# A graph network layer on one core: TensorE's instructions written as loops, and a ring of 48 gathered tiles instead of 50

## The reference, cut to what matters

```python
def mish(x): return x * jnp.tanh(jax.nn.softplus(x))
sent = nodes[senders]                                # one row of 128 for each of 50000 edges
e = mish(sent + edges @ W_e_k + W_e_b)
agg = jax.ops.segment_sum(e, receivers, num_segments=n)
h = (1.0 + eps) * nodes + agg
...
# layers 1 and 2 sum neighbours again over the same src, dst:
agg = jax.ops.segment_sum(h[src], dst, num_segments=n_nodes)
```

## Time and profile before

| | us |
|---|---|
| median of 3 runs | 2208.66 |
| lowest, highest | 2203.86, 2209.03 |
| the profiled execution, its own time | 2216.36 |
| its span, first to last instruction | 2214.6 |
| build, first to last product of line 685 (about) | 75 to 485 |
| edges, first word of line 699 to last (about) | 494 to 938 |

### The profile page before, as it was taken

One profiled execution on the slowest core, in us unless ns is written; L12 is line 12 of the kernel. 1 busy time (PEld: TensorE's weight loads), 2 busy tenths in 40 slices (PEclk: granted clock), 3 DMA queues, 4 the chain that ended last, 5 costly groups with the idle time before them and its releaser, 6 DMA issues. The chain is left out here.

```text
span 2214.6 us, 31367 instructions
## 1 busy us (share of the span) xinstructions
PE 1322.1 (60%) x7890; PEld 1079.8 (49%) x7890; DVE 1066.3 (48%) x2950; ACT 944.2 (43%) x2004; POOL 1037.5 (47%) x1171
## 2 busy tenths in 40 slices
PE   3222146666676689799989997314444454434666
PEld 2100013444554578688989895214433453424555
DVE  4411149873443467554964315314444454433666
ACT  0100137774454468275536645413333343333424
POOL 5677710005566640024458441665565666556234
PEclk9555569988888789999989998657676777667787
DMA  5221212224565563074545451546667666666521
GB/s 147 70 66 53 68 55 104 90 99 152 166 197 162 169 211 101 11 252 164 194 136 208 147 209 49 162 135 172 172 184 197 199 187 197 177 169 176 157 67 43
DMA packets 214072, 314.19 MB, mean 142 GB/s; under 512 B 31232, under 2 KB 159743, under 8 KB 213818
## 3 DMA queue, kind: packets, MB, share of 16 engines
q1 hardware_dynamic: 110724, 153.96, 21.9%
q0 software_dynamic: 33488, 81.02, 13.0%
q10 hardware_dynamic: 69734, 77.65, 10.9%
HBM read 223.87 MB, written 88.67 MB: 141 GB/s over the span
## 5 line engine op out<-in xcount | busy, mean ns | idle before, releaser
L374 POOL DMA_INDIRECT fr_ring<-table,src_i x392 | 376.2, 960 | 405.5 <-SPq L655 277.7
L1765 POOL DMA_INDIRECT e_kv<-kv_table,e_idx x392 | 387.1, 987 | 269.0 <-DVE e_msg L1848 153.7
L685 PE MATMUL fe_ps<-fe_space 128*128 128x400 bf16 x591 | 176.0, 422 | 244.5 <-issue 151.9
L685 PEld LDWEIGHTS fe_ps<-fe_space 128*128 128x128 bf16 x591 | 86.0, 145 | 334.3 <-issue 309.2
L776 DVE TENSOR_SCALAR fe_space<-fe_space,fr_key 128x400 bf16<-128x400 f16 x591 | 157.5, 323 | 176.1 <-remote 77.7
L1004 POOL CAST ly_af<-ly_au 128x640 fp32r<-128x640 uint16 x240 | 163.4, 729 | 126.4 <-DVE ly_part L1409 61.0
L1779 PE MATMUL e_q<-e_qs,e_mask 128*128 128x136 f32 x784 | 148.1, 360 | 80.9 <-issue 48.2
L1831 ACT ACTIVATE e_row<-e_p 128x864 f32<-128x864 f32 x56 | 49.6, 885 | 336.4 <-remote 292.5
L731 ACT ACTIVATE fe_space<-fe_ps 128x800 uint16<-128x800 f32 x100 | 83.6, 836 | 255.8 <-PE fe_ps L685 140.0
L707 PE MATMUL fe_ps<-fr_ring,fe_space 128*128 x976 | 147.9, 294 | 61.7 <-issue 32.3
L1779 PEld LDWEIGHTS e_q<-e_qs,e_mask 128*128 128x128 f32 x784 | 135.6, 258 | 87.9 <-issue 81.2
(11 more groups left out here) (397 smaller groups left out, 3177.2 us busy)
## 6 DMA issues: line engine op xcount, KB each, us to landing
ly_au<-edge_counts SPq DMA_DIRECT2D x88, 800.0 KB, 4.5
sums_att<-e_row ACTq DMA_DIRECT2D x56, 532.0 KB
q_starts<-fe_space SPq DMA_DIRECT2D x56, 476.0 KB
e_qs<-q_starts SPq DMA_DIRECT2D x56, 476.0 KB
fe_edge<-in_edgesT ACTq DMA_DIRECT2D x98, 256.0 KB
edge_counts<-fe_space ACTq DMA_DIRECT2D x25, 800.0 KB
e_drow<-dst_short SPq DMA_DIRECT2D x56, 224.0 KB
fr_ring<-table,src_i POOLq DMA_INDIRECT x392
```

The source lines that it names most:

```text
L374: pool.indirect_dma_start(f.ring[:, n % RB, t, 0:D], None, tab[0][:, :], bass.IndirectOffsetOnAxis(ap=src_i[:, at:at + 1].bitcast(U32), ax ...
L685: nc.tensor.matmul(ps[:, bass.ds(at, NW)], left(n), right(n % IS), start=False, stop=True, skip_group_check=True).then_inc(c["item"], 1)
L1765: pool.indirect_dma_start(kv[s][:, t, :], None, kv_table[:, :], bass.IndirectOffsetOnAxis(ap=idx[s][:, t:t + 1].bitcast(U32), axis=0)).the ...
```

## The change

`RB` goes from 50 to 48. The number of semaphores over which gathers are spread, `SB`, goes from 7 to 12; the number of tiles gathered beside the tables stays 7 (`SF`), and GpSimd's wait for an earlier tile on the same semaphore starts with tile 12. TensorE's build becomes a loop of 5 turns over 16 groups (112 items), with the 5 last groups written out. TensorE's edges become 12 items written out, a loop of 6 turns over 12 items (i from 12 to 83) and the last 38 items written out (i from 84 to 121). Inside a loop the word's place, the counts waited for and the place in the ring are computed in registers. No engine's work on data changes.

```diff
-SB = 7
-RB = 50
+SB = 12
+SF = 7
+RB = 48
+PU = 12
...
-                        for n in range(SB, NF):
+                        for n in range(SF, NF):
                             if n >= RB:
                                 pool.wait_ge(released, n - RB + 1)
-                            pool.wait_ge(f.fetched_in[n % SB], n // SB * 16 * TF)
+                            if n >= SB:
+                                pool.wait_ge(f.fetched_in[n % SB], n // SB * 16 * TF)
...
-                        for g in range(WGS):
-                            word = pe.value_load(f.bank_words[0:1, g:g + 1])
+                        def group(word, items):
+
                             turn = nc.s_assert_within((word >> TURN_BITS) & 255, 1, BLOCKS)
                             pe.wait_ge(c["taken"], turn)
-                            for k in range(min(WG, ITEMS - g * WG)):
-                                n = g * WG + k
+                            for k, (n, made) in enumerate(items):
                                 at = (word // 8 ** k) % 8 * BANK if k < WG - 1 else (turn + 7) % 8 * BANK
-                                c.ready(pe, "hot", n)
+                                pe.wait_ge(c["hot"], made)
                                 nc.tensor.matmul(ps[:, bass.ds(at, NW)], left(n), right(n % IS),
                                                  start=False, stop=True, skip_group_check=True).then_inc(c["item"], 1)
...
+                        turns = ITEMS // (2 * IG * WG)
+                        with pe.Fori(0, turns) as r:
+                            for g in range(2 * IG):
+                                group(pe.value_load(f.bank_words[0:1, bass.ds(r * (2 * IG) + g, 1)]),
+                                      [(g * WG + k, r * (2 * IG * WG) + (g * WG + k + 1)) for k in range(WG)])
+                        for g in range(turns * 2 * IG, WGS):
+                            group(pe.value_load(f.bank_words[0:1, g:g + 1]),
+                                  [(n, n + 1) for n in range(g * WG, min(ITEMS, (g + 1) * WG))])
...
-                        for i in range(FI):
-                            item(i)
-                            if i + AHEAD < NF:
-                                pre(i + AHEAD)
+                            pre_of(n)
+                        for i in range(PU):
+                            item_of(i)
+                        with pe.Fori(1, NF // PU - 1) as r:
+                            for k in range(PU):
+                                item(k, pe.value_load(f.take_words[0:1, bass.ds(r * PU + k, 1)]), r * PU + (k + 1), r * PU + (k - 2))
+                                n, q = (k + AHEAD) % PU, (k + AHEAD) // PU
+                                slot = nc.s_assert_within((r + q) % (RB // PU) * PU + n, 0, RB - 1)
+                                pre(n, ring[:, bass.ds(slot, 1), :, 0:D].rearrange("p n t f -> p (n t) f"), r + (q + 1),
+                                    r * (PU // ER) + ((k + AHEAD) // ER + 1), r * PU + (k + AHEAD - PR + 1))
+                        for i in range((NF // PU - 1) * PU, FI):
+                            item_of(i)
```

More of the change, by code:

```diff
@@ L74 @@
 NC = -(-E // HEAVY)
+assert PU % SB == 0 and PU % ER == 0 and PU % PR == 0 and PU % NH == 0 and RB % PU == 0 and RB // PU == 4 and PU >= 3
 assert TM == TB - 1 and NB % KS == 0 and KS % ES == 0 and NT % NS == 0 and EP >= E and ET == TK * TP
@@ L437, in _ @@
                                   allow_small_or_imprecise_dtypes=True).then_inc(counted, 1)
-                        for n in range(SB):
+                        for n in range(SF):
                             fetch(pool, f, n)
@@ L683, in _ @@
                                 at = (word // 8 ** k) % 8 * BANK if k < WG - 1 else (turn + 7) % 8 * BANK
-                                c.ready(pe, "hot", n)
+                                pe.wait_ge(c["hot"], made)
                                 nc.tensor.matmul(ps[:, bass.ds(at, NW)], left(n), right(n % IS),
                                                  start=False, stop=True, skip_group_check=True).then_inc(c["item"], 1)
-                        def pre(n):
-                            pe.wait_ge(f.fetched_in[n % SB], (n // SB + 1) * 16 * TF)
-                            c.free(pe, "msg", n, PR)
-                            nc.tensor.matmul(bank_of(n), ident[:, :], ring[:, n % RB, :, 0:D], start=True, stop=True)
-                            pe.wait_ge(landed[n % ER], (n // ER + 1) * 16)
+                        turns = ITEMS // (2 * IG * WG)
@@ L693, in pre @@
+                        def pre(n, tile, turn, edges, read):
+                            pe.wait_ge(f.fetched_in[n % SB], turn * (16 * TF))
+                            if read is not None:
+                                pe.wait_ge(c["msg"], read)
+                            nc.tensor.matmul(bank_of(n), ident[:, :], tile, start=True, stop=True)
+                            pe.wait_ge(landed[n % ER], edges * 16)
                             for t in range(TF):
@@ L696, in pre, with item @@
                             last.then_inc(c["pre"], 1)
-                        def item(i):
-                            word = pe.value_load(f.take_words[0:1, i:i + 1])
+                        def item(i, word, made, read):
                             needed = nc.s_assert_within((word >> 16) & 127, 1, NF)
                             at = nc.s_assert_within(word % 65536, 0, (RB - 1) * TF * RW1)
-                            c.ready(pe, "hot_n", i)
-                            c.free(pe, "add_n", i, 3)
+                            pe.wait_ge(c["hot_n"], made)
+                            if read is not None:
+                                pe.wait_ge(c["add_n"], read)
                             pe.wait_ge(c["msg"], needed)
@@ L708, in item, with pre_of, item_of @@
                             last.then_inc(c["item_n"], 1)
+                        def pre_of(n):
+                            pre(n, ring[:, n % RB, :, 0:D], n // SB + 1, n // ER + 1, n - PR + 1 if n >= PR else None)
+                        def item_of(i):
+                            item(i, pe.value_load(f.take_words[0:1, i:i + 1]), i + 1, i - 2 if i >= 3 else None)
+                            if i + AHEAD < NF:
+                                pre_of(i + AHEAD)
                         pe.wait_ge(c["taken"], 8 + BLOCKS)
                         for n in range(AHEAD):
-                            pre(n)
-                        for i in range(FI):
-                            item(i)
-                            if i + AHEAD < NF:
-                                pre(i + AHEAD)
+                            pre_of(n)
[10 more added lines that the diff above has]
+                            item_of(i)
                     @block.scalar
```

## The result

The changed kernel takes 2258.73 us (median; 2255.22 to 2278.27), the kernel before in the same comparison 2206.26 us (2198.66 to 2209.03). The ratio is 1.026, 95% interval 1.023 to 1.029: 2.6% slower, where 2171 us and a gain were forecast. The profiled execution took 2256.01 us, with a span of 2254.3 us, 39.7 us more than the profiled execution before.

A forecast was written before the change was run, and what follows sets the result against it. TensorE was taken to be short of instructions while GpSimd gathers, the edges' stops belonging to first-run code. Build +40, edges -93 and longer pairs +15 sum to -38 us: 2208.66 to 2171 us, bounds 2140 to 2205.

The forecast's parts named there:

- The build while gathers run: TensorE's build until 300 us: still first-run code, loop gives nothing; 34-instruction groups take 23.8 us, 64 items done there.
- one instruction in 0.70 us, whatever it is: Build's slow stretch: TensorE gets any instruction only every 0.70 us, so 26 in a group make 18.2 us.
- The build after that: Build after the gathers: added register instructions at 0.1 us make groups 3.1 instead of 2.4 us, +40 us (ends 0 and +75).
- The edges while gathers run: TensorE's edges: first 24 items lose the same 55 us; looped items 24 to 83 lose nothing, -93 us.
- The longer pairs: Edges' loop: 52.8 instructions instead of 49 in each of 72 pairs, +15 us (ends 0 and 29).
- Ring and semaphores: GpSimd's gathers: 12 semaphores for 7 and 48 ring places for 50 change nothing.
- The rivals: Three other outcomes: starving loops (chance 0.29), hidden register instructions (0.12), the build's slow stretch cured too (0.07).
- The first, that resident code starves as well: Edges' loop: stops stay, 0 instead of -93, and 10% more instructions in them add 15 us; 2279 us, chance 0.29.
- The rule of the Trainium skill cited there: Instructions stream in blocks of 256; branches outside a two-page window force a fetch, so both loop bodies would be refetched each turn.

## Why the prediction was wrong

**The build while gathers run.** Its end (300 us) and its being unaffected by the loop held. The group was mis-sized: 28 us, not 23.8. The count of instructions, 34, was right, but the rule "one instruction in 0.70 us, whatever it is" was not: 26 x 0.70 fitted 18.2 us by coincidence, and what counts are the sequencer's rows at 1.40 us, 13 before and 20 after. The interval between two rows was in the trace of before.

**The build after that.** Held: 3.1 us a group, 0.09 us for each register instruction, end some 5 us later than forecast (+46 instead of +40 for the build), because about 76 items and not 86 were done by 300 us. Two kernels show this cause: six register instructions added, and five taken away together with five waits.

**The edges while gathers run.** This step failed, and it decides the result: -93 us for items 24 to 83, measured -6 for them and -2 for all of the edges. The stops do not belong to code that is run for the first time; they come with unbroken gathers, in code just run as well. It rested on the earlier trace rows, that q8 brings new code, and on the earlier trace rows, that TensorE does not starve in the attention's loop. The first was a coincidence of two facts: all code was new where TensorE starved, because all code of this stage was written out. The run with no gather in the build shows new code at full speed, and the second to fifth turn of the edges' loop show code already run with stops. The second took the length of TensorE's own rows for a proof that it loses nothing. Those rows are at full speed in the worst stretch of all too, where the news of a product is 43 us late. And in the attention's loop SyncE has rows up to 1407 ns, against 37 on the chip where nothing starves, and TensorE waits 157.5 us for VectorE, against 2.1 there. So TensorE loses time in that loop as well. How much of it is starving no run took apart.

**The longer pairs.** Forecast +15, measured 0: with no gathers in the way the loop's pair takes 2.65 us, as before. The bound 0 was the right one.

**Ring and semaphores.** Nothing, as forecast: the kernel with the edges' loop, the ring of 48 and the 12 semaphores gives 0.997, with an interval that includes 1. The three were not taken apart.

**The rivals.** The first, that resident code starves as well, is what happened; it gave 2279 us, of which the 15 us for pairs did not come and the 15 us of longer stops neither: 2208.66 + 46 = 2255. Part of that is luck: its evidence, VectorE's 46-instruction loop at 2.8 us an item, is no case of resident code that is slow. VectorE's own rows of line 776 take 57 ns in the starved stretch:

```profile
L776 DVEq FUSED_REGOPS  x23: 53/57/64, 242.6 to 303.5; - x23
```

What it waits for is TensorE's count of items. VectorE writes item m when product m - 8 is done. From 160 to 305 us it starts 14 to 22 us after that product's end, from 314 us on within 1.4 us. It is the late news again.

The rule of the Trainium skill cited there ("Runtime: NRT & Kernel Launch", "Instruction fetch mechanics") is not borne out for these bodies: 546 and 634 instructions were not fetched anew in each turn, q8 fell from 64 to 46 packets. The same section of the Trainium skill gives TensorE's instruction memory as 128 KiB or 2048 instructions, which the prediction passed over; both bodies fit in that, and q8's fall agrees with it. Its advice, to write the code out, agrees with the result, but for another reason: the register instructions.

**What stays open.** What in a gather holds up the other engines' rows and the news of TensorE's products, whether these two are one thing, and why it happens on some chips and not on another (or beside what else ran near them), no run here tells.

## What to carry to other kernels

When a stretch is slow by "issue" and register instructions stand at 0.7 us, look for the engine that works without a break, and move or pace its work before touching the slow engine's code; one run with that work moved elsewhere tells more than any reading of the waits. Rows at full speed do not clear an engine: compare the end of a product with the start of what waits for it on another engine. A slow code that is also new code is no proof that it is slow for being new: look for the same stops where the code has been run before. And before a rule such as "so many instructions at 0.70 us" is carried over to another program, measure the interval between single rows; a sum that fits once can fit by chance. And count a loop's register instructions, since each between two short products costs about 0.1 us on a sequencer that sets the pace, some 50 us here.

## What the runs showed of the hardware

- While GpSimd gathers without a break, one gather in 1.25 us, TensorE's sequencer rows can take 0.70 us and start 1.40 us apart (before: 13 in 18.2 us; changed kernel: 20 in 28.0 us).
- In the same condition VectorE and ScalarE can see a product of TensorE as done 43.4 us after its end, with TensorE's own register rows at 36 ns: 7 items in 224 us (gathers behind the build). The longest such lag is 16.2 us in the first profile's edges and 0.5 us on the chip where nothing starves.
- A pause after every four gathers ends or nearly ends it: 2.8 us of waiting (kernel 5% shorter) or 0.8 us of other work (9% shorter, a single run).
- It depends on the chip or on what is near it. The same program took 2208 to 2223 us on three chips (numbers 8, 0 and 13; 2206 us in the first comparison, whose chip is not on record) and 1714 to 1715 us, 22% less, on a fourth (number 5), in two sets of runs. 800 numbers of other work after each tile gain 9% on chip 13 and lose 7% on chip 5.
- A register instruction ahead of a product costs 1.4 us in the starved build and about 0.09 us otherwise (2.54 to 3.16 us for seven more in a group; 3.16 to 2.72 us for five fewer, with five waits); in the edges' pairs, where TensorE is busy throughout, nothing (2.65 us a pair with and without).
- A body of 634 instructions stayed resident on TensorE: q8 brought nothing from 653 to 917 us of the changed kernel's edges. In the build's loop of 546 it brought one packet between 240 and 552 us.
